# Transposes of `a` and of the next `h` side by side in a gated MoE kernel, with a seven-row ring and moved small products

## The reference

```python
def _L0_xattn_ref(hidden_states, token_ids, Wg, Wu, Wd):      # all three are ctx
    for e in range(E):                                         # E = 4, chosen by the token's id
        g = silu(einsum('bsd,fd->bsf', hidden_states, Wg[e]))
        u = einsum('bsd,fd->bsf', hidden_states, Wu[e])
        y = einsum('bsf,df->bsd', g * u, Wd[e])
        out = where(expert_ids == e, y, out)
def _L0_ffn_ref(x, gate_W, W1, b1, W2, b2):
    gate_probs = softmax(einsum('bd,ed->be', x.mean(axis=1), gate_W))
    topk_vals, topk_idx = top_k(gate_probs, 2)                 # renormalised
    h = gelu(einsum('bsd,bkdf->bksf', x, W1[topk_idx]) + b1)
    return einsum('bk,bksd->bsd', topk_vals, einsum('bksf,bkfd->bksd', h, W2[topk_idx]) + b2)
x = x + tanh(g_xattn) * _L0_xattn_ref(layernorm(x), ids, ctx, ctx, ctx)
x = x + tanh(g_ffn) * _L0_ffn_ref(layernorm(x), gate_W, W1, b1, W2, b2)
```

## Time and profile before

| | |
|---|---|
| time, median of 3 runs | 287.7 us (286.22 to 288.25) |
| the profiled execution | 287.67 us, of which its span is 285.9 us |
| PE busy | 277.8 us (97%), 1395 matmuls and transposes |
| DVE busy | 218.8 us (77%) |
| ACT, POOL busy | 117.1 us (41%), 70.5 us (25%) |
| chain that ended last | PE 93%, DVE 3%, ACT 2% |

### The profile page before, as it was taken

One profiled execution on the slowest core, in us unless ns is written; L12 is line 12 of the kernel. 1 busy time (PEld: TensorE's weight loads), 2 busy tenths in 40 slices (PEclk: granted clock), 3 DMA queues, 4 the chain that ended last, 5 costly groups with the idle time before them and its releaser, 6 DMA issues.

```text
span 285.9 us, 4480 instructions
## 1 busy us (share of the span) xinstructions
PE 277.8 (97%) x1395; PEld 224.8 (79%) x1395; DVE 218.8 (77%) x499; ACT 117.1 (41%) x200; POOL 70.5 (25%) x113
## 2 busy tenths in 40 slices
PE   8969999999999999999999998999999999999995
PEld 5858888888888888887788876788788877888884
DVE  8696988788778899689986758978777677867173
ACT  4742423222232223472637265372753746625020
POOL 5455064555454545443232000000000000000000
PEclk9988999999999999999999999999999999999999
DMA  6770023222227223229702405961096602940003
GB/s 216 246 255 24 2 74 110 75 76 75 90 97 221 76 79 106 75 74 270 231 37 79 144 0 166 262 232 62 5 285 216 215 0 82 326 167 0 2 0 147
DMA packets 24018, 35.00 MB, mean 122 GB/s; under 512 B 4120, under 2 KB 12318, under 8 KB 23996
## 3 DMA queue, kind: packets, MB, share of 16 engines
q1 hardware_dynamic: 20928, 24.72, 27.4%
q0 software_dynamic: 3040, 9.98, 10.7%
q10 hardware_dynamic: 28, 0.02, 0.0%
HBM read 25.52 MB, written 9.19 MB: 121 GB/s over the span
## 4 chain that ended last, share of the span: by engine, by line
PE 93%; DVE 3%; ACT 2%; issue 1%; ACTq 0%
PE bank L1121 38%; PE bank L1095 12%; PE bank L1097 12%; PE bank L1096 12%; PE bank L1173 3%; PE bank L1112 3%; PE bank L1103 3%; PE bank L1237 2%; PE bank L1307 1%; PE bank L1308 1%; PE bank L1063 1%; PE bank L1277 1%; DVE x_odd L832 1%; PE bank L1276 1%; PE bank L1059 1%
## 5 line engine op out<-in xcount | busy, mean ns | idle before, releaser
L1095 PE MATMUL bank<-w_lo,ctx_hi 128*128 128x512 f32 x80 | 31.6, 395 | 0.0
L1097 PE MATMUL bank<-w_hi,ctx_lo 128*128 128x512 f32 x80 | 31.2, 390 | 0.0
L1096 PE MATMUL bank<-w_hi,ctx_hi 128*128 128x512 f32 x80 | 31.2, 389 | 0.0
L914 ACT ACTIVATE aT_hi<-bank 128x512 fp32r<-128x512 f32 x18 | 10.8, 599 | 40.4 <-PE bank L1112 38.4
L984 ACT ACTIVATE w_hi<-w_raw 128x512 fp32r<-128x512 f32 (+3 forms) x24 | 23.9, 1020 | 5.8 <-DMA w_raw<-in_L_ffn_W 5.7
L919 ACT ACTIVATE a<-bank 128x512 f32<-128x512 f32 x19 | 11.4, 598 | 35.5 <-PE bank L1121 35.5
L1121 PE MATMUL bank<-ctx_hi,hT_hi 128*128 (+1 forms) x80 | 24.3, 426 | 0.9 <-ACT hT_hi L909 0.9
L991 ACT ACTIVATE act<-bank,tables 128x512 f32<-128x512 f32 x16 | 11.0, 688 | 31.8 <-PE bank L1097 31.7
L1095 PE MATMUL bank<-ctx_lo,w_hi 128*128 128x512 f32 x60 | 23.6, 393 | 0.0
L1096 PE MATMUL bank<-ctx_hi,w_hi 128*128 128x512 f32 x60 | 23.4, 390 | 0.0
L1097 PE MATMUL bank<-ctx_hi,w_lo 128*128 128x512 f32 x60 | 23.3, 389 | 0.0
(11 more groups left out here) (214 smaller groups left out, 611.0 us busy)
## 6 DMA issues: line engine op xcount, KB each, us to landing
raw_ctx<-in_ctx SPq DMA_DIRECT2D x4, 1024.0 KB, 8.1
w_raw<-in_L_ffn_W SPq DMA_DIRECT2D x8, 512.0 KB, 4.9
x_even<-x_scratch SPq DMA_DIRECT2D x8, 257.0 KB, 3.7
x_odd<-x_scratch SPq DMA_DIRECT2D x8, 257.0 KB, 3.1
w_raw<-in_L_ffn_W SPq DMA_DIRECT2D x8, 256.0 KB, 4.1
out<-x_even SPq DMA_DIRECT2D x8, 256.0 KB, 2.2
out<-x_odd SPq DMA_DIRECT2D x8, 256.0 KB, 2.1
w_raw<-in_L_ffn_W SPq DMA_DIRECT2D x4, 448.0 KB
```

What stands on the lines that cost most here:

```text
L914: sc.activation(aT_hi[:, :, :].rearrange("p k t -> p (k t)"), aT_ps[:, :], ACT.Copy).then_inc(aT_hi_done, 1)
L1095: pe.matmul(dst, s_hi, m_lo, start=first, stop=False)
L1096: pe.matmul(dst, s_hi, m_hi, start=False, stop=False)
L1097: return pe.matmul(dst, s_lo, m_hi, start=False, stop=last)
```

## The change

There are six edits.

- **Transposes.** From step 5 on (`PAIRED`) `transpose_h(j+1)` stands right behind `transpose_a(j-1)`, and `first_product(j)` and `second_product(j-1)` follow without transposes between them. DVE's order in these steps becomes `a_low`, the add of `residual` (now `add`), `rows_statistics(j+2)`, the statistics of the finished tile (`statistics`), `up(j)`, `normalise(j+2)`, `h_low(j+1)`: a row is normalised at the end of the step ahead. From step 12 on the add stands ahead of `a_low`.
- **Ring.** `RING` is 7, one more tile is gathered early, and POOL's power for tile j+4 stands ahead of the scatter of tile j in the paired steps. The tables `below` and `early` move into memory that is used later.
- **Step 15.** `logits(0)` stands ahead of `transpose_a`, and the wait for `neg_max_ready` behind `transpose_a`.
- **Second part.** In `hidden(0, 1)` `logits(1)` stands behind the sixth matmul of the first block, and `spread_mix(b+1)` behind the third block for every b.
- **Warm-up at the start.** The seven products of 512 columns become thirty of 128 columns.
- **Warm-up ahead of the first tile.** Nine transposes without use stand ahead of `transpose_h(0)` and five behind it, into the bank of z, with a wait for `tg_done`.

```diff
-    WARM = (7, 10)
+    WARM = (30, 10, 9, 5)
-    RING = 6
+    RING = 7
+    PAIRED = range(E + 1, TILES)
@@ POOL
+            for j in range(1, TILES):
+                paired = j + 2 in PAIRED or j + 3 in PAIRED
+                if paired and j + AHEAD < TILES:
                     inverse_root(j + AHEAD)
                 scatter(j, j % RING)
+                if not paired and j + AHEAD < TILES:
+                    inverse_root(j + AHEAD)
                 landed(j - 1)
@@ DVE, steps up to 11
+                if j in PAIRED or j + 1 in PAIRED:
+                    if j not in PAIRED:
+                        normalise(j + 1)
+                    add(j - 2, y_ps)
+                    rows_statistics(j + 2)
+                    statistics(j - 2)
+                    up(j)
+                    normalise(j + 2)
+                    h_low(j + 1)
@@ PE, start
+            pe.wait_ge(tg_done, 1)
+            warm_up(WARM[2], z_ps)
             transpose_h(0)
+            warm_up(WARM[3], z_ps)
             first_product(0, 0, lambda: transpose_h(1))
@@ PE, tile step
                 transpose_a(j - 1)
+                if j in PAIRED:
+                    transpose_h(j + 1)
                 first_product(j, e)
-                transpose_h(j + 1)
+                if j not in PAIRED:
+                    transpose_h(j + 1)
                 second_product(j - 1, e_before)
@@ PE, hidden
                         last = hidden_block(b, s, c, k)
+                        if more and b == 0 and n == 0 and k == 1:
+                            logits(b + 1)
                     last.then_inc(hid_done, 1)
-                    if more and b == 0 and n == 0:
-                        logits(b + 1)
-                    if more and n == (1 if b == 0 else 0):
+                    if more and n == FC - 1:
                         spread_mix(b + 1)
@@ PE, steps from 12 on
-                transpose_a(j - 1)
                 if j == PREP + 3:
                     logits(0)
-                first_product(j, e)
+                transpose_a(j - 1)
                 if j == PREP + 3:
                     pe.wait_ge(neg_max_ready, 1)
                 if j + 1 < TILES:
                     transpose_h(j + 1)
+                first_product(j, e)
```

More of the change, by code:

```diff
@@ L230, in flamingo_kernel @@
         part = sb("part", [P, 1])
-        below = sb("below", [P, P], BF16)
-        early = sb("early", [P, P], BF16)
+        below = table(P // 2).bitcast(BF16)
+        early = table(P // 2).bitcast(BF16)
         ones_h = sb("ones_h", [P, P], BF16)
@@ L636, in rows_statistics, with add @@
                 dve.tensor_scalar(ve1[:, :], mv1[:, 1:2], EPS, None, ALU.add).then_inc(ve_ready, 1)
-            def residual(j, bank=y_ps):
+            def add(j, bank):
                 dve.wait_ge(y_done, j + 1)
@@ L646, in residual @@
                 dve.tensor_tensor(ring_row(j, D, 2), mv2[:, :], eps_row[:, :], ALU.add).then_inc(x1_ready, 1)
+            def residual(j, bank=y_ps):
+                add(j, bank)
+                statistics(j)
             def normalise(j):
@@ L720, in _ @@
                 a_low(j - 1)
[L721 to L726, removed]
+                if j in PAIRED or j + 1 in PAIRED:
[7 more added lines that the diff above has]
+                    h_low(j + 1)
+                else:
+                    if j > 2:
+                        normalise(j + 1)
+                        residual(j - 2)
+                    h_low(j + 1)
+                    up(j)
+                    rows_statistics(j + 2)
             def ffn_normalise(b, ts=range(TT)):
@@ L840, in _ @@
                     scale_logits(0)
+                add(j - 2, y_ps)
                 a_low(j - 1)
-                if j + 1 < TILES:
-                    normalise(j + 1)
-                residual(j - 2)
+                if j + 2 < TILES:
+                    rows_statistics(j + 2)
+                statistics(j - 2)
                 if j == PREP + 4:
                     mixing(0)
+                up(j)
+                if j + 2 < TILES:
+                    normalise(j + 2)
                 if j + 1 < TILES:
                     h_low(j + 1)
-                up(j)
-                if j + 2 < TILES:
-                    rows_statistics(j + 2)
                 if j < PREP + 2:
@@ L1055, in _, with warm_up @@
         def _(pe):
-            def warm_up(count):
+            def warm_up(count, bank=o_ps[3]):
                 for _ in range(count):
-                    pe.transpose(o_ps[3][:, 0:P], ident[:, :], ident[:, :])
+                    pe.transpose(bank[:, 0:P], ident[:, :], ident[:, :])
             pe.wait_ge(ones_made, 1)
             for _ in range(WARM[0]):
-                pe.matmul(o_ps[3][:, :], ones_h[:, :], ones_h[:, :].unsqueeze(1).to_broadcast([P, 4, P]), start=True, stop=True)
+                pe.matmul(o_ps[3][:, 0:P], ones_h[:, :], ones_h[:, :], start=True, stop=True)
             pe.wait_ge(consts_made, 4)
@@ L1326, in _ @@
                     transpose_h(j + 1)
+                first_product(j, e)
+                if j + 1 < TILES:
                     if j == PREP + 2:
```

17 lines of the change are left out of this document (4 added, 13 removed).

## The result

The changed kernel takes 283.25 us (median; 283.16 to 283.62) against 287.81 of the kernel before beside it. The ratio is 0.9858, with a 95% interval from 0.9821 to 0.9895: 1.4% less. The profiled execution took 283.31 us, of which the span is 281.3.

A forecast was written before the change was run, and what follows sets the result against it. TensorE's work, clock and few waits were taken as the bound. 287.67 less 1.5 (warm-up), 0.3 (pairs), 0.4 (gate's steps), 0.8 (entry 1), plus 0.15, and some 0.1 for small ends, gave 284.7 us; range 283.3 to 286.7.

The forecast's parts named there:

- What bounds the kernel: Whole kernel: TensorE sets the pace, so gains must come from its own work, its clock or its few waits.
- The warm-up ahead of the first tile: Before the first tile: fourteen more transposes keep the clock up and delay nothing, a gain of 1.5 us.
- The thirty short products: At the start: they take about as long as the seven long ones, cost 0, with 2.8 us as other end.
- The far end of 2.8 us: At the start: if each short product pays 0.20 us for its weight load, everything up to `h` is 2.8 us late.
- Transposes side by side: Paired steps: eight transposes together save 0.02 us a step, 0.3 us over thirteen steps; bounds 0 and 0.8.
- DVE's new order: Paired steps: `h_low` ends 0.45 us before TensorE needs it, cost 0; step 4 is 0.15 us late once.
- The slower rival: Paired steps: VectorE becomes the bound once `h_low` needs over 0.45 us extra; 288.6 us at 0.75, chance 0.06.
- The gate's steps: Two steps forming the gate: 0.9 us of waiting for a late `normalise` gives way to 0.5, a gain of 0.4.
- The second wait, the new one: Second step with the gate: TensorE waits 0 to 0.55 us for `h_low`, taken as 0.5.
- The gate of batch entry 1: Second part: waits of 0.68 and 0.24 us go, 0.2 comes back; 0.8 us gained, bounds 0.4 and 1.1.
- the rival with more gain: Tile steps: pairs save their upper bound and the gate's new wait is 0, giving 283.7 us; chance 0.15.
- the delayed start: At the start: short products expose their weight loads, up to 2.8 us, giving 287.5 us; chance 0.08.

The follow-up runs named there:

- transposes apart: Changed kernel with TensorE's and VectorE's old order in the tile steps, two groups of four transposes per tile again: 283.97 us.
- the start alone: Kernel before with only the changed start: thirty short products and the nine and five transposes; 285.35 us, 0.9938 of the kernel before.
- eight long products: Changed kernel with eight warm-up products of 512 columns in place of thirty of 128: 283.32 us.
- late statistics: Changed kernel with statistics of the tile two back moved behind `h_low` in the step where mixing stands: 282.44 us, 0.9833 of the kernel before.
- VectorE's work added: Changed kernel with the first statistics instruction of a tile's rows doubled, 0.72 us more VectorE work in twelve paired steps: 287.04 us.

## Why the prediction was right or wrong

**What bounds the kernel** was right: TensorE's own work, its clock and a few waits. All that was gained came from these three, and the loop gained nothing from VectorE's new order except where TensorE had waited.

**The warm-up ahead of the first tile** was right in kind: no fall of the clock, and 1.96 us to `transpose_h(1)`, where 1.9 was forecast. The 1.5 us are there (2.85 - 1.35). The prediction took the fall for a property of the kernel; it is one of some executions only, 41 of 57 before and 4 of 10 without the fourteen transposes. With these and without the pause at 4.2 us, none of 30 executions showed it (of the changed kernel, taken twice, transposes apart, the start alone, eight long products and late statistics); only with VectorE's work added did two of ten have a mean granted clock of 0.992 and 0.994.

**The thirty short products** are the step that failed. They were priced as a delay, and that price, 0, is right: the counts come at 4.29 us, 4.32 before. That they would lift the clock 3 us earlier, worth 1.35 us in the profile, was no term at all. The question that was not asked is what TensorE does between the end of the seven products, 4.22, and the counts: it idles for 0.1 us by the modelled end, 0.3 by the starts. In the three profiles with seven long products the clock rose at 9.25 to 10.17 us; in the eight in which TensorE went into the counts with a pause of at most 0.07 it rose at 3.85 to 6.11. The ranges do not overlap, and eight long products do as well as thirty short ones; that it is the pause, and not an eighth product's work, stays argued. The Trainium skill, in TensorE: Matmul & The Clock Gate, Part 1: The HAM clock gate, says that the moment of the rise varies from run to run for the same kernel; the trace agrees, with 6.11 and 5.59 us in the two profiles of the changed kernel. Two of the eight rises (3.85 and 4.27) come ahead of the counts, where seven long products run as well, which fits the three quick executions with seven. The far end of 2.8 us took the 0.20 us of the transposes at 7.17 for loads that show; it is the pace of the slow clock, for in the changed kernel transposes of this size stand 0.21 us apart ahead of the rise and 0.11 behind it.

**Transposes side by side**: 0.056 us a step (6.406 less 6.35), not 0.02. The upper bound, which let the matmuls behind each product's start run faster too, was the nearer: it gave 0.06. Step 5 lost 0.08 once, where 0.15 was forecast. Steps 1 to 13 gained 0.39; the forecast for all thirteen paired steps was 0.15 net.

**DVE's new order** costs nothing, as forecast: spare 0.45 forecast, 0.51 by the experiment with more work. The slower rival had its threshold right, and nothing took up the spare.

**The gate's steps**: a gain of 0.4 was forecast, 0.1 came (14.04 for 14.14). The first wait went, as forecast, but not for the reason given. The prediction put 0.9 us of the old steps down to a late `normalise`; these are the rows of the kernel before (L1103 is the transposes of `h`, L642 the add):

```profile
127.28 1.07 PE L1121 MATMUL bank<-ctx_hi,hT_lo 128*128 x4
128.01 0.74 DVE L642 SCALAR_TENSOR_TENSOR x_ring<-bank,tg,x_ring 128x512 f32<-128x512 f32 x1
128.18 0.63 PE L1103 MATMUL bank<-ident,h 128*128 128x128 f32 x4
128.90 1.17 PE L1121 MATMUL bank<-ctx_hi,aT_hi 128*128 x4
...
135.53 0.66 PE L1103 MATMUL bank<-ident,h 128*128 128x128 f32 x4
136.28 1.17 PE L1121 MATMUL bank<-ctx_hi,aT_hi 128*128 x4
```

In the first of the two steps the transposes of `h` come in time, 0.90 us after the four matmuls ahead of them. What is late is the second product, 0.72 us behind the transposes where 0.35 is usual. It writes the bank that the add reads, and the add ends at 128.75, 0.15 us ahead of it. In the second step `normalise` costs some 0.2 us, and the second product is again late, 0.75 us behind the transposes and 0.15 behind the end of the add (136.13). The same 0.15 stands in both steps of the three other runs with the old order; in steps 13 to 15 the add is done some 0.5 us ahead, or more. So some 0.7 of the 0.9 was a wait for the add, which the change puts ahead of `a_low` in these steps; there it ends at 124.08, ahead of the second product at 125.29. No run moves the add alone.

The second wait, the new one, was forecast at 0.5 and cost 0.90. `h_low` ended 7.94 us into the step (129.62 less 121.68), beyond even the bound of 7.8. The 6.53 us of work are those of the old step, at whose end `rows_statistics` (1.02 us) runs over into the next one, so that half of one is inside; in the new order a whole one stands ahead of `h_low`. `normalise` also took 0.73 us there, where it took 0.54 before. To the end of `h_low` VectorE is busy for 7.22 us and idle for 0.72, where the prediction had 6.53 and 0.61. The experiment with late statistics shows that 1.0 us out of that chain removes all of it. The logits of step 15 cost nothing, as forecast (14.97 for the steps 14 and 15, 15.05 before).

**The gate of batch entry 1**: 1.18 us in place of 0.8, just past the upper bound of 1.1. The mechanism and the 0.2 that came back at the third block (0.18) were right. The prediction's own terms, 0.68 and 0.24 less 0.2, make 0.72 and not 0.8. The waits were mis-sized, since their price was read from the brackets. In the kernel before, these matmuls stand ahead of the two waits:

```profile
171.44 0.39 PE L1279 MATMUL bank<-h2T_hi,w_hi 128*128 128x512 f32 x1
...
178.37 0.39 PE L1097 MATMUL bank<-w_hi,ctx_lo 128*128 128x512 f32 x1
```

The row at 179.00 has a bracket of 0.24, but the matmul ahead of it started at 178.37, so the distance is 0.63 where 0.23 is usual: 0.40. A matmul's modelled end lies 0.16 behind the point at which the next could start, and the bracket counts from that end. The wait of 0.68 likewise: 1.07 from the start ahead of it (171.44) to 172.51, where `spread_mix` without a wait takes 0.32 (171.08 to 171.40 after): 0.75. Less the 0.18 that came back, the two make 0.97; the other 0.2 comes in pieces of 0.1 us or less along the second part.

**The sum.** Forecast were 3.0 us, and 4.4 came in the profiled execution (287.67 less 283.31): 1.35 more at the start, 0.24 more by the pairs, 0.2 less in the steps with the gate (0.18 for 0.4, the logits' gain among it), 0.4 more in the second part; the 0.1 of small ends did not come, and the time around the span is 2.0 us in place of 1.8. By the medians of the experiments the start gives 1.8, the second part 1.6 (285.78 for 287.42) and the pairs 0.7, 4.1 together; the first two medians hang on how many executions with a fall were among those taken, and like against like the second part gives 1.2 to 1.3. The time is nearest to the rival with more gain (283.7), but not for its reason: the pairs did reach its bound, while the gate's wait went the other way.

**The rivals.** The clock dropped in no execution of the changed kernel; the delayed start did not come, and VectorE did not become the bound.

## What to carry to other kernels

Where a warm-up fills the beginning, try one that reaches without a break into the work that follows it, and price it by what it does to the clock, not only by what it may delay. Take several executions before a single profile's clock is called the kernel's. Take a wait's price from the distance between the starts on either side less the usual distance, not from the idle time alone. Look up which instruction frees what a late product writes before a wait is put down to its inputs. When a step's order is turned round, write the chain of the engine that is now last anew from its real start, with what runs over from the step ahead.

## What was not expected of the hardware

- A pause of 0.1 us by the modelled end (0.3 by the starts) on TensorE at 4.2 us goes with a clock that rises 3 to 6 us later, in three profiles against eight. With no products at all it rose at 7.80 in one profile, earlier than with seven and the gap (9.25 to 10.17 in three).
- The same kernel has executions with and without a fall of the clock, some 2.6 us apart (medians of 285.2 and 287.9 us among 25 executions of the kernel before); the fall explains only some 1.1 to 1.5 us of that. Idling of 2.60 and 0.69 us just ahead of the first matmuls did not bring a fall in the execution that was profiled.
- ScalarE begins four copies of `ctx_hi` up to 1.95 us after the work ahead of them without a row that says why, in some executions of the same kernel (0.15 and 0.52 in the other profile of it). It moves the first tile by up to 1.2 us.
